# A macaron block (FFN, attention, FFN) on one core: the attention's row maxima six groups ahead of its scores instead of seven, the first FFN's shared tile last, the first batch loaded beside it

## The reference

```
x = x + 0.5 * FFN(layernorm(x))        # layer 0 of the kernel's FFN code
x = x + ATT(layernorm(x))
x = x + 0.5 * FFN(layernorm(x))        # layer 1, same weights

FFN: route = sigmoid(x @ router_w); each token goes to its best of 8 experts
     h = silu(x @ gate_w[e]) * (x @ up_w[e]);  out = (h @ down_w[e]) * route[e]     # 256 -> 512 -> 256
ATT: 16 query heads of 16, 4 groups of key/value heads, causal softmax over 256 keys, scale 1/4
```

## Time and profile before

| | us |
|---|---|
| median of 3 runs | 416.62 (414.96 to 417.93) |
| the profiled execution, its time | 416.29 |
| its span, first to last instruction | 414.5 |
| mean granted PE clock | 0.978 of full speed |

### The profile page before, as it was taken

One profiled execution on the slowest core, in us unless ns is written; L12 is line 12 of the kernel. 1 busy time (PEld: TensorE's weight loads), 2 busy tenths in 40 slices (PEclk: granted clock), 3 DMA queues, 4 the chain that ended last, 5 costly groups with the idle time before them and its releaser, 6 DMA issues.

```text
span 414.5 us, 8450 instructions
## 1 busy us (share of the span) xinstructions
PE 374.9 (90%) x3164; PEld 294.5 (71%) x3171; DVE 243.0 (59%) x732; ACT 143.7 (35%) x296; POOL 175.3 (42%) x288
## 2 busy tenths in 40 slices
PE   8999999999998698888999999998699999999980
PEld 6769999999673455555566665555399999989660
DVE  5889852222222647778878778889757874222220
ACT  3221111111110234565767657577334111111110
POOL 1041425552111254556767664565812215643111
PEclk9999999999999979999999999999989999999996
DMA  8959932299103524202213042200211101398000
GB/s 266 409 207 351 333 106 76 66 334 333 40 16 114 156 81 126 56 20 78 78 48 105 20 121 71 55 28 28 59 57 37 43 25 56 103 345 318 27 23 14
DMA packets 27055, 50.04 MB, mean 121 GB/s; under 512 B 4458, under 2 KB 20590, under 8 KB 25975
## 3 DMA queue, kind: packets, MB, share of 16 engines
q1 hardware_dynamic: 19118, 25.10, 18.7%
q0 software_dynamic: 4512, 21.50, 15.1%
q10 hardware_dynamic: 3376, 2.80, 2.3%
HBM read 35.16 MB, written 6.55 MB: 101 GB/s over the span
## 4 chain that ended last, share of the span: by engine, by line
PE 67%; DVE 17%; DMA 5%; issue 4%; SPq 3%; ACT 1%; another core or an unknown queue 1%; POOL 1%; POOLq 0%; DVEq 0%; ACTq 0%
PE bank L1003 25%; PE bank L1024 13%; PE bank L1228 3%; PE bank L1457 3%; PE bank L1485 3%; PE bank L1386 2%; PE bank L542 2%; DVE mxa L1416 2%; PE bank L993 2%; PE bank L965 2%; PE bank L1514 2%; SPq L1333 1%; PE bank L1379 1%; DVE area L1534 1%; PE bank L592 1%
## 5 line engine op out<-in xcount | busy, mean ns | idle before, releaser
L1003 PEld LDWEIGHTS bank<-area,W 128*128 128x128 f32 x1024 | 119.9, 193 | 3.5 <-ACT area L1093 1.7
L1003 PE MATMUL bank<-area,W 128*128 128x128 f32 x1024 | 120.9, 277 | 1.2 <-ACT area L1093 1.2
L1172 DVE TENSOR_TENSOR area<-area,bank 128x512 f32<-128x512 f32 x34 | 23.4, 687 | 71.5 <-issue 49.7
L1464 ACT ACTIVATE area<-bank 128x512 f32<-128x512 f32 x96 | 54.2, 597 | 27.8 <-PE bank L1457 27.4
L1024 PE MATMUL bank<-W,area 128*128 128x256 f32 x256 | 60.9, 381 | 1.8 <-DVE area L1157 1.8
L1473 POOL TENSOR_SCALAR_AFFINE_SELECT area<-area 128x512 f32<-128x512 f32 x64 | 40.8, 650 | 40.5 <-ACT area L1464 40.2
L1104 ACT ACTIVATE area<-bank 128x512 f32<-128x512 f32 x34 | 20.3, 597 | 97.1 <-PE bank L1003 87.5
L1024 PEld LDWEIGHTS bank<-W,area 128*128 128x128 f32 x256 | 46.2, 190 | 7.9 <-issue 2.9
L1416 DVE TENSOR_REDUCE mxa<-bank 128x2 f32<-128x512 f32 x64 | 42.9, 673 | 7.2 <-PE bank L1388 7.1
L892 POOL DMA_INDIRECT out<-area,sidx x17 | 17.1, 1005 | 55.3 <-DVE area L1157 52.6
L892 POOL DMA_INDIRECT x2d<-area,sidx x17 | 17.1, 1006 | 54.7 <-DVE area L1157 54.7
(11 more groups left out here) (200 smaller groups left out, 574.3 us busy)
## 6 DMA issues: line engine op xcount, KB each, us to landing
W<-wall SPq DMA_DIRECT2D x24, 512.0 KB, 8.8
area<-area SPq DMA_DIRECT2D x48, 128.0 KB, 2.4
area<-x SPq DMA_DIRECT2D x8, 256.0 KB, 5.3
area<-x2d SPq DMA_DIRECT2D x8, 256.0 KB, 4.6
rows<-area ACTq DMA_DIRECT2D x8, 256.0 KB, 2.5
area<-JV SPq DMA_DIRECT2D x40, 32.0 KB, 1.9
cb<-constb ACTq DMA_DIRECT2D x1, 296.0 KB, 4.4
area<-x,gidx POOLq DMA_INDIRECT x18, 3.5
```

The costliest lines, as they stand in the source:

```text
L1003: last = pe.matmul(ps[:, i * P:(i + 1) * P], W[:, w:w + P], xT[:, j % 2, c, :], start=(c == 0), stop=(c == C - 1))
L1172: v.tensor_tensor(out, sil[:, n % 2, :], bank[2 + n % 2][:], ALU.mult).then_inc(f_h[l], 1)
L1464: a.activation(PT[:, n % 2, u * 512:(u + 1) * 512], bank[u][:], ACT.Exp, scale=D ** -0.5).then_inc(a_e, 1)
```

## The change

The shared tile of layer 0 moves to position 16, the last; layer 1 keeps it at 15. In layer 0 its gate and up products are cut so that `ffn_down` of position 15 stands after the first quarter. SP loads batch 0 when the last up product is done and the scatters of positions 0 to 15 have landed; batches 1 to 7 wait for `s_fin` as before. DVE normalises batch 0 right after `finish` of the last tile. The groups of statistics are batch 0, batch 1, batches 2 to 4 (were 0, 1 to 3, 4), the third with its Newton steps on DVE, which also normalises batch 2; the guess for the inverse root takes one DVE instruction less. Four groups of maxima stand ahead of group 0's scores; iterations 0 and 1 hold two groups each (4, 5 and 6, 7), iteration n from 2 on group n+6. Batch 0's maxima are sent in halves of 8 heads. `a_neg_dve` of the next batch stands at the end of g = 1, its `a_neg_pe` and `a_neg_copy` in g = 2. `warm` calls: 12 and 20 instead of 48, 8, 3 and twelve of one. The last `ffn_down` of layer 1 writes bank 7 instead of bank 6. What is left out of the diff below hands `l` on to `tile_of`, `mixed` and `mixed_before`, and follows the same edits on other lines.

```diff
-MIX = 15
+MIX = (2 * NE, 2 * NE - 1)
...
-WARM_MID = 48
+WARM_MID = 12
+WARM_NEXT = 20
...
-        LN_GROUPS = (((0, BA), (BA, B)), ((0, 1), (1, 4), (4, 5)))
+        LN_GROUPS = (((0, BA), (BA, B)), ((0, 1), (1, 2), (2, BA)))
...
-            link(nc.vector.tensor_scalar(hv[:, t0:t1], ve[:, t0:t1].bitcast(I32), 1, None,
-                                         ALU.arith_shift_right), seen)
-            nc.vector.tensor_scalar(rs[:, t0:t1], hv[:, t0:t1], -1.0, RSQRT_MAGIC,
+            nc.vector.tensor_scalar(rs[:, t0:t1], ve[:, t0:t1].bitcast(I32), -0.5, RSQRT_MAGIC,
...
+        def shared_gate_up(l, m, chunks):
+            pe = nc.tensor
+            j = MIX[l]
+            if m == 0 and 0 in chunks:
+                pe.wait_ge(s_sw, 16 * NQ * (l + 1))
+                pe.wait_ge(f_xs[l], j + 1)
+                pe.wait_ge(f_si[l], j - 1)
+                pe.wait_ge(f_h[l], j - 1)
+            ps = bank[2 * m + j % 2]
+            for c in chunks:
+                w = (m * C + c) * I
+                for q in range(NQ):
+                    last = pe.matmul(ps[SUB * q:SUB * q + SUB, :], xT[:, j % 2, c, SUB * q:SUB * q + SUB],
+                                     stage[:, q, w:w + I], start=(c == 0), stop=(c == C - 1),
+                                     tile_position=(0, SUB * q))
+            if C - 1 in chunks:
+                last.then_inc((f_gp, f_up)[m][l], 1)
+        def down_bank(l, n):
+            return bank[7] if l == 1 and n == NP - 1 else bank[6]
...
+            if n >= 1 and down_bank(l, n) is bank[6]:
                 pe.wait_ge(f_o[l], n)
...
+                    shared_gate_up(l, 0, (0,))
+                    if j == NP - 1:
+                        ffn_down(l, j - 1, offs[j - 1])
+                    shared_gate_up(l, 0, (1,))
+                    shared_gate_up(l, 1, (0, 1))
...
+            if MIX[l] == NP - 1:
+                ffn_transpose_hidden(l, NP - 1)
...
+                if j == MIX[l] == NP - 1:
+                    finish(j - 1)
                 hidden(j)
...
             finish(NP - 1)
+            if l == 0:
+                first_norm(seen)
...
+        def row_batch(e):
+            return max(e - 1, 0)
+        def rows_sent(b):
+            return 16 * (b // QB + 1 + (b % QB == 0))
+        def a_max_row(sp, e):
+            r = row_batch(e) % QB
+            h0, h1 = ((0, NH // 2), (NH // 2, NH))[e] if e < 2 else (0, NH)
+            sp.wait_ge(a_ms, e + 1)
+            sp.dma_start(Qs[MROWS:MROWS + 1, r, h0:h1].rearrange("o h s -> o (h s)"), mT[h0:h1]).then_inc(a_mq[r], 16)
...
+        def maxima(n):
+            return (NG + 2 * n, NG + 2 * n + 1) if n < 2 else (n + NG + 2,)
...
+        def a_neg_dve(e):
...
+            b = row_batch(e)
+            v.wait_ge(a_am, 3 * NG // 2 if e == 0 else 3 * NG * (b + 1))
+            if e >= 1:
+                v.wait_ge(a_mp, e)
+            h0, h1 = ((0, NH // 2), (NH // 2, NH))[e] if e < 2 else (0, NH)
+            v.tensor_scalar(nmx[:, :, h0:h1], mxa[:, b % 2, :, h0:h1], -1.0, None, ALU.mult).then_inc(a_nm, 1)
...
+        def a_neg_copy(e):
...
+            v.wait_ge(a_mp, e + 1)
+            if e == 1:
+                v.wait_ge(a_mq[0], 16)
+            elif e >= 2:
+                v.wait_ge(a_mq[(b - 1) % QB], rows_sent(b - 1))
+            v.tensor_copy(mT[0:n], bankm[0:n, 0:S]).then_inc(a_ms, 1)
...
-            if g == 0 and u == 0:
-                pe.wait_ge(a_mq[r], 16 * (b // QB + 1))
+            if u == 0 and (g == 0 or n == NG // 2):
+                pe.wait_ge(a_mq[r], 16 if n == 0 else rows_sent(b))
...
-            sp.wait_ge(s_fin[0], 1)
+            sp.wait_ge(f_up[0], NP)
+            for i in range(OB):
+                sp.wait_ge(f_s[0][i], 16 * (2 * NE // OB))
             for b in range(B):
+                if b == 1:
+                    sp.wait_ge(s_fin[0], 1)
                 sp.dma_start(xt[:, TB * b:TB * b + TB, :],
...
-            a_stack_shared(sp, 0)
-            a_stack_shared(sp, 1)
-            a_stack(sp, 2, (0, 1))
+            a_stack_q(sp, 0, 0)
+            a_stack_k(sp, 0, 0, slice(1, 3))
+            a_stack_q(sp, 0, 1)
+            a_stack_q(sp, 0, 2)
+            a_stack_q(sp, 1, 0)
+            a_stack_k(sp, 1, 0, slice(2, 3))
+            a_stack_q(sp, 1, 1)
+            a_stack_q(sp, 1, 2)
+            a_stack_k(sp, 1, 2)
             a_max_row(sp, 0)
-            a_stack(sp, 2, (2,))
+            a_stack(sp, 2, (0,))
+            a_max_row(sp, 1)
+            a_stack(sp, 2, (1, 2))
             for b in range(B):
                 if b + 1 < B:
-                    a_max_row(sp, b + 1)
+                    a_max_row(sp, b + 2)
                 if b + 3 < B:
                     a_stack(sp, b + 3)
...
-            ln_apply(2, p)
-            ln_apply(3, p)
             a_split_dve2(1, p)
             a_split_dve3(1, p)
+            ln_apply(3, p)
             a_split_dve2(2, p)
+            a_mask(0)
             a_split_dve3(2, p)
-            ln_newton(1, 2, seen)
-            a_mask(0)
...
+            a_split_act(0, PRO_Q[0])
+            a_split_act2(0)
+            a.wait_ge(s_fin[0], 1)
+            a_stack_k(a, 0, 0, slice(0, 1))
+            a_split_act3(0)
+            a_stack_k(a, 0, 1)
+            a_vt_act(0, PRO_KV[0])
+            a_stack_k(a, 0, 2)
+            ln_evacuate(1, 1, PRO_T[1])
+            a_split_act(1, PRO_Q[1])
+            a_split_act2(1)
+            a_stack_k(a, 1, 0, slice(0, 2))
...
             for u in range(3):
                 a_exp(0, u)
+            a_split_act3(2)
...
+                if n == 0:
+                    ln_evacuate(1, 3, PRO_T[3])
...
-            for t in range(*tiles(1, 0)):
-                ln_sums(1, t, seen)
-            ln_stats(1, 0, seen)
-            ln_newton(1, 0, seen, v)
-            ln_apply(0)
             for t in range(*tiles(1, 1)):
                 ln_sums(1, t, seen)
             ln_stats(1, 1, seen)
-            v.wait_ge(s_const, 2)
+            a_split_k(0, PRO_KV[0])
+            a_split_dve2(0)
...
-            ln_apply(1)
-            a_split_dve(0, PRO_KV[0])
-            a_split_dve2(0)
-            a_split_dve3(0)
+            v.wait_ge(s_const, 2)
+            a_split_v(0, PRO_KV[0])
             ln_stats(1, 2, seen)
-            a_split_dve(1, PRO_KV[1])
-            for m in range(NG + 3):
-                for u in range(3):
-                    a_max_dve(m, u)
-                if m == 2:
-                    a_split_k(2, PRO_KV[2])
-                if m == 3:
-                    a_split_v(2, PRO_KV[2])
-                    a_neg_dve(0)
-                    a_neg_copy(0)
+            ln_newton(1, 2, seen, v)
+            a_split_k(1, PRO_KV[1])
+            ln_apply(2)
+            for m in range(NG):
+                for k in range(3):
+                    a_max_dve(m, k)
+                    if (m, k) == (0, 2):
+                        a_split_v(1, PRO_KV[1])
+                    if (m, k) == (1, 2):
+                        a_neg_dve(0)
+                    if (m, k) == (2, 0):
+                        a_neg_copy(0)
+                        a_split_k(2, PRO_KV[2])
+                    if (m, k) == (3, 0):
+                        a_split_v(2, PRO_KV[2])
+            a_neg_dve(1)
...
+                own = maxima(n)
+                m, more = own[0], m_left(n)
...
+                if g == 2 and b + 1 < B:
+                    a_neg_copy(b + 2)
...
-                if g == 1 and b + 1 < B:
-                    a_neg_copy(b + 1)
...
-                if g == 2 and b < B - 2:
-                    round_half(b, seen)
-                if g == 0 and b + 1 < B:
-                    a_neg_dve(b + 1)
+                for x in own[1:]:
+                    for k in range(3):
+                        a_max_dve(x, k)
+                if g == 1 and b + 1 < B:
+                    a_neg_dve(b + 2)
...
+            warm(WARM_NEXT)
             ln_transpose(1, 1, PRO_T[1])
             a_vt_pe(0, PRO_KV[0])
-            warm(8)
...
-            a_vt_pe(1, PRO_KV[1])
-            warm(3)
-            for m in range(NG + 3):
-                for u in range(3):
-                    a_max_pe(m, u)
-                    if 2 <= m <= NG + 1:
-                        warm(1, bank[0])
-                    if (m, u) == (0, 1):
+            for m in range(NG):
+                for k in range(3):
+                    a_max_pe(m, k)
+                    if (m, k) == (0, 1):
                         ln_transpose(1, 2, PRO_T[2])
-                    if (m, u) == (0, 2):
+                        a_vt_pe(1, PRO_KV[1])
+                    if (m, k) == (0, 2):
                         pe.wait_ge(a_q32, 1)
+                        a_proj_q(2, PRO_Q[2], (0,))
+                    if (m, k) == (1, 0):
+                        a_proj_q(2, PRO_Q[2], (1,))
+                    if (m, k) == (1, 1):
                         pe.wait_ge(a_v, 1)
                         pe.wait_ge(a_k32, 1)
```

(91 more changed lines are left out.)

134 lines of the change are left out of this document (52 added, 82 removed).

## The result

The changed kernel takes 421.76 us (median of 11 runs, 418.95 to 423.14), the kernel before 417.45 beside it: 1.0085 times as long, with an interval of 1.0057 to 1.0112. The medians alone give 1.0103, the recorded ratio a little less. A run more than 1.5% above the fastest of its kernel, as one of before with 548 us, counts in no ratio. The forecast was 411.5, and its range ended at 417.5; the ratio stays under the 1% that the prediction took as no change. The profiled execution took 422.87 us for a span of 421.1, which is 6.6 more than the 414.5 before.

A forecast was written before the change was run, and what follows sets the result against it. From 125 to 171 us a chain of DVE, POOL, ACT and DMA steps was taken as the bound, in the loop PE. −9.3 + 3.7 − 0.5 + 2.0 − 0.7 = −4.8 from 416.29 gave 411.5; range 405.5 to 417.5.

The forecast's parts named there:

- Part 5: Loop, new order in g = 2: PE waits for DVE's negated maxima, +3.7 (0 to 8.4); batch 7's stack wait goes, −0.5.
- Part 2: Prologue, batch 1: ready at 138.6, −4.8; first maxima product at 144 instead of 154.19, −10.
- Part 3: Prologue, four groups of maxima ahead of the scores: first scores at 156.3 instead of 170.67, −14.4.
- Part 3's sign: Prologue: DVE comes to its first reduction at 145.8; being far from that would show the prediction wrong.
- part 1: Start of batch 0: early load and normalising, done at 130.5 instead of 136.96, −6.5.
- Part 3's half row: Prologue: the half row leaves DVE at 153.4 and lands 1.8 to 2.2 later, in time for the first scores.
- Part 4: Three put-off groups in iterations 0, 1 and 25: iterations 0 and 1 take 7.2 and 7.3; lead −9.3 at iteration 3.
- part 6: The ends: iteration 25 with group 31 costs +2.0 (1.1 to 3.6); second FFN's last down products, −0.7.
- Rival 3: Loop: the row of maxima is late for every batch; slower, 422 with 2 us more on DVE; chance 0.07.
- Rival 2: Prologue gives less: PE at 1.2 GHz as long as before, or DVE's queue delays the first reduction; 415, chance 0.25.
- Rival 4: Batch 0's early load doesn't bring batch 1 forward and the put-off groups eat the rest; 417, chance 0.06.
- The rule that I weighed: Prologue, maxima stretch 144 to 157: taking filler away risks the slow clock; as a warning, rival 2's time.

The follow-up runs named there:

- e1: The changed kernel with five warm matmuls in g = 2 ahead of PE's wait for the negated maxima; 416.67 us, 0.9996 of before.
- e12: The changed kernel with five warm matmuls, the second splits behind the negation, and loads of batches 5 to 7 behind batch 0's stacks; 409.53 us, 0.9833 of before.
- e4: The changed kernel with the loads of batches 5 to 7 issued behind batch 0's stack DMAs; 417.53 us, 1.0052 of before.
- e10: e6 with the first half of batch 0's row negated, copied and sent only behind the four groups of maxima; 411.61 us, 0.9905 of before.
- e5: The changed kernel with the old loop order, maxima seven groups ahead and groups 4 to 6 behind the first scores; 410.89 us, 0.987 of before.
- e3: The kernel before with only the changed loop order: maxima six groups ahead, negated maxima transposed and copied in g = 2; 429.3 us, 1.027 of before.
- e2: The changed kernel with DVE's second split of k and q behind the negation at the end of g = 1; 418.57 us, 1.0053 of before.
- e6: e5 with the loads of batches 5 to 7 issued behind batch 0's stack DMAs; 405.74 us, 0.9759 of before.

## Why the prediction was wrong

**Part 5 is the step that failed.** It said "I take 0.75 for each of four batches", 3.0 of its +3.7, and the loop from iteration 3 to group 19, which holds these four, cost 7.3 (−2.65 to +4.67), 1.8 a batch. The mechanism was right: PE waits for DVE at `a_neg_pe`, the scores and values queue behind. The price of the wait was nearly right as well: 0.9 by e1, where 0.75 stood, though the wait itself is 1.7 and not "up to 1 us". What was left out is PE's clock: behind the wait PE runs part of the batch at the lower level in three of the four batches, another 1.4 each time. The clock was weighed as a risk of the prologue only; in the loop I took full clock for granted because before had it throughout. The upper end, 1.4 a batch, was passed in the batches where the clock fell (2.3 to 2.5); only the sum over six, 8.4, holds the 7.3, and that is luck.

**Part 2 is the second, and in us the larger:** of the 11.4 us between forecast (−4.8) and profile (+6.6), 4.3 are part 5's and 6.65 had arisen by iteration 3 (−2.65, where −9.3 stood). "Batch 0's twelve stack DMAs are out by 140.4 and landed before that": SP issued its share of them from 138 to 143, and they landed up to 7.0 us later. The step counted SP's order of issue and each DMA's price when alone, but not the traffic beside them (a DMA share of 1.00). Of the 5.6 us by which the first maxima product was late (149.64 against 144), the stack wait is 3.8; batch 1, normalised at 141.56 instead of 139.4, is the rest. What makes the stack DMAs slow stays open, as said under e12, and batch 1's lateness (the first FFN's end is 0.7 later, the last-scatter signal 1.45 later than forecast) is read from the trace and not tested.

Part 3's sign, DVE's first reduction at 145.8, failed too: it came at 150.49. DVE was ready for it at 148.66, 2.9 late, and then waited 1.84 for PE's product; so without the stack wait 1.8 us and not 3.8 would have been saved there. From the first reduction to the first scores it took 12.4 us where the forecast had 10.5. e4, the same program from there on but with a granted clock of 1.00, took 9.9, so the 1.2 GHz stretch cost some 2.5. The first scores came at 162.86, not 156.3: −7.8 instead of −14.4.

**Right were:** part 1, batch 0 normalised at 130.96 (130.5). Part 3's half row: PE doesn't wait for its DMA, and e10 shows what sending it late costs. Part 4, +5.15 for the put-off work (+5.1), and not by luck: iteration 0 took 7.20 us (7.2), with DVE's wait of 2.32 for PE in it, and iteration 1 7.54 (7.3); but e5 shows that putting it off bought next to nothing. Behind group 19, where 0.7 and −0.5 of part 5 and 2.0 of part 6 make 2.2, the loop cost 1.7. Of the second FFN the 0.63 us wait ahead of the last down products is gone, as the chain of after shows (last two lines below), yet the FFN is 0.2 longer and not 0.7 shorter, which its spread over the profiles hides:

```profile
308.85 5.68 PE bank L990 x32
...
406.03 1.86 PE bank L1031 x32
407.90 1.94 PE bank L1035 x8
```

The first line is that FFN's first gate and up stage: 5.68 us, where before the same view has 4.49. Its first 3 us ran at a granted 0.50; before, 302 to 305 had 0.62.

The sum: −2.65 at iteration 3, +7.3, +1.7 and +0.2 are 6.55, the 6.6 of the spans.

**The rivals.** None gave the result. Rival 3, the one on the slower side, had the right place, the chain from negation to row, but the row was in time: its DMAs took 3.6 at most and PE waited for one once, 0.3. What came late was one step earlier, the negation itself. Rival 2's clock fall in the prologue happened, 6.4 us of it, and alone would have led to about 415. Rival 4's half happened: batch 1 came 2.65 earlier and not 4.8. Nothing combined it with part 5, and so 0.07 was left for slower. The rule that I weighed, that activity releases the slow clock (the Trainium skill, "TensorE: Matmul & The Clock Gate", Part 1: The HAM clock gate), agrees with three stretches: 149.6 to 156 in after, 162 to 174 in e10, and the loop, where five warm matmuls a batch bring the clock from 0.94 to 1.00. Filler taken away is only a risk, though: e4 has as little of it as after and keeps 1.00 from 140 to 160.

## What to carry to other kernels

A wait put on PE can cost more than itself: through the clock behind it 0.9 us became 2.3 to 2.5 in the loop's batches in which it fell, and 2.9 became 6.0 in e10; price both, and fill a wait that can't be avoided. Moving a step one iteration nearer its use, to shorten a prologue, exposes whatever stands in the slower engine's queue in every iteration after: here 9 us lost for 0.3 gained. A stage started earlier may run into transfers that it used to follow: count what else is in flight when a small DMA is on the path. Bulk loads issued behind such DMAs gained 1.1% and 1.3% here, but didn't make them fast in every trace.

## What was not expected of the hardware

- A wait of 1.7 us in a batch of 18, with PE 90% busy, can lower the granted clock, but need not: in after it did so at 217 and 237 and not at 198, with the same 1.70 us. Over three batches the clock is 0.94 (after), 0.91 (e3, e2) and 1.00 with five warm matmuls in the wait (e1).
- Stack DMAs that land in 2.4 us in the median took up to 7.0 (after), 8.9 (e5) and 9.2 (e12). In e12 three of the seven loads of 256 KB were behind them, in e6 as well, and there the slowest took 3.4. What decides stays open.
- A wait without a releaser need not be a riddle: DVE's 2.32 us at 169 in after is the 2.35 us for PE's L1418 in e1, whose trace has the record that after's lacks.
- e1 and e2 change nothing in the prologue, and yet their first scores come 2.0 and 2.8 us earlier than after's, with stack waits of 3.1 and 2.9 us instead of 3.8. Why a profile differs so from the next stays open; it is a reason to read the loop by its period and not by the end.
